# Layer-1 gathers moved into the drain and the stream's last step, and a wait for landing behind every fourth gather

## The reference

```python
def layer0(h, input, adj, weight):              # M = N = 6144, D = 128
    scores = where(adj > 0, einsum('md,de,ne->mn', h, weight, input), NEG_PAD)
    return softmax(scores / 0.07, axis=1) @ input

def layer1(h, W, a, adj):
    h = h @ W
    e = leaky_relu((h @ a[:128])[:, None] + (h @ a[128:])[None, :], 0.2)
    valid = (adj > 0) & (h.sum(axis=1) != 0)[None, :]
    att = where(valid, softmax(where(valid, e, -1e9), axis=1), 0)
    # entries under THR dropped, scaled by the number of valid neighbours
    return elu(h + attention @ h)

h = relu(layernorm(x)); x = x + layer0(h, ...)
h = relu(layernorm(x)); x = x + layer1(h, ...)
```

## Time and profile before

| | |
|---|---|
| median of 3 runs | 885.34 us (879.32 to 888.77) |
| the profiled execution's own time | 888.49 us |
| its span, first to last instruction | 886.7 us |
| mean granted TensorE clock | 0.717 of full speed |
| busy: PE, DVE, ACT, POOL | 420.1, 538.7, 389.0, 327.0 us |
| DMA packets' share of 16 engines, hardware and software queue | 49.6%, 10.7% |

### The profile page before, as it was taken

One profiled execution on the slowest core, in us unless ns is written; L12 is line 12 of the kernel. 1 busy time (PEld: TensorE's weight loads), 2 busy tenths in 40 slices (PEclk: granted clock), 3 DMA queues, 4 the chain that ended last, 5 costly groups with the idle time before them and its releaser, 6 DMA issues. The chain is left out here.

```text
span 886.7 us, 9190 instructions
## 1 busy us (share of the span) xinstructions
PE 420.1 (47%) x2773; PEld 274.2 (31%) x2806; DVE 538.7 (61%) x2015; ACT 389.0 (44%) x395; POOL 327.0 (37%) x358
## 2 busy tenths in 40 slices
PE   2356465757575656666646464632024010006564
PEld 0013223433333243434333243432023000006564
DVE  0087767767777778786859577885125020018995
ACT  4487766666575667665656624420001000001222
POOL 4003242423333232417172725556721777720000
PEclk9568786887887878696888877856555555556867
DMA  9999978878787788888979872311211222211222
GB/s 337 423 420 399 360 282 315 294 282 301 281 339 277 303 275 330 282 325 243 349 249 334 285 265 77 91 31 39 54 23 55 52 55 55 54 22 37 73 73 86
DMA packets 38037, 186.75 MB, mean 211 GB/s; under 512 B 7904, under 2 KB 9184, under 8 KB 19424
## 3 DMA queue, kind: packets, MB, share of 16 engines
q1 hardware_dynamic: 28768, 167.02, 49.6%
q0 software_dynamic: 9216, 19.11, 10.7%
HBM read 179.73 MB, written 6.37 MB: 210 GB/s over the span
## 5 line engine op out<-in xcount | busy, mean ns | idle before, releaser
L853 ACT ACTIVATE arena<-arena,half_c 128x2048 bf16<-128x2048 int32 x144 | 282.8, 1996 | 51.3 <-DMA arena<-in_adj 50.4
L788 POOL DMA_INDIRECT X<-in_L_gnn_input,idx_all x138 | 142.3, 1031 | 363.4 <-DVE idx_near L1094 325.0
L1430 PE MATMUL K<-arena,bits 128*128 128x512 bf16 x546 | 189.1, 478 | 143.6 <-ACT arena L853 130.5
L1430 PEld LDWEIGHTS K<-arena,bits 128*128 128x128 bf16 x576 | 60.6, 115 | 230.9 <-ACT arena L853 149.8
L809 POOL DMA_INDIRECT arena<-table,idx_near x96 | 91.0, 948 | 62.2 <-DMA table<-hs 33.3
L1019 DVE MAX8 keys<-K 128x8 int32<-128x128 f32 x192 | 42.5, 284 | 79.0 <-PE K L1430 70.7
L809 POOL DMA_INDIRECT E<-table,idx_near x48 | 48.8, 1016 | 14.5 <-issue 13.4
L881 ACT CAST R_all<-G 128x512 fp8e4<-128x512 f32 (+1 forms) x37 | 19.9, 575 | 69.1 <-PE G L1463 69.1
L988 ACT ACTIVATE above<-above,zero_c 128x24 f32<-128x24 f32 x6 | 1.9, 314 | 100.5 <-DVE above L1360 100.5
L1441 PE MATMUL G<-g,R_all 128*128 128x128 bf16 x333 | 32.7, 273 | 20.4 <-issue 16.0
L874 ACT CAST g<-W 128x512 bf16<-128x512 f32 (+1 forms) x13 | 7.2, 550 | 76.2 <-remote 73.9
(11 more groups left out here) (235 smaller groups left out, 995.9 us busy)
## 6 DMA issues: line engine op xcount, KB each, us to landing
arena<-in_adj SPq DMA_DIRECT2D x144, 1024.0 KB
E<-in_L_gnn_input SPq DMA_DIRECT2D x1, 3072.0 KB, 23.4
table<-hs SPq DMA_DIRECT2D x11, 262.0 KB
hs<-table SPq DMA_DIRECT2D x11, 262.0 KB, 2.8
x_all<-in_x SPq DMA_DIRECT2D x1, 2816.0 KB, 17.6
out_x<-x_all SPq DMA_DIRECT2D x11, 256.0 KB, 2.0
X<-in_L_gnn_input,idx_all POOLq DMA_INDIRECT x138
arena<-table,idx_near POOLq DMA_INDIRECT x96
```

The source lines that it names most:

```text
L788: pool.indirect_dma_start(out=x_of(b)[:, e, :], out_offset=None, in_=inp, in_offset=bass.IndirectOffsetOnAxis(ap=idx_all[:, at:at + 1], ax ...
L853: nc.scalar.activation(sign[:, load % RING, :], ring[:, load % RING, :], ACT.Sign, bias=half_c[:], scale=1.0).then_inc(signed, 1)
L1430: last = mm(bank_[:], bits[:, third * TB + j, :], sign[:, load % RING, j * FOLD:(j + 1) * FOLD], start=False, stop=(third == G - 1 and j = ...
```

## The change

Behind every fourth gather Pool waits until that gather, and those before it on its semaphore, have landed. This holds in `neighbours` and in `records`. The order of `records` changes: `records(0, 4)` goes into step 12, `records(1, 0)` and `records(1, 1)` go ahead of the last two `mean` and the last `neighbours`, the rest of third 1 and `records(0, 5)` go ahead of the wait for the whole of table 2, and only the six of third 2 stand behind it.

```diff
+    FEW = 4
...
                         ).then_inc(X_r[b], 16)
+                        if e % FEW == FEW - 1:
+                            pool.wait_ge(X_r[b], 16 * (e + 1))
...
                         ).then_inc(E_r[g][i], 16)
+                        if t % FEW == FEW - 1:
+                            pool.wait_ge(E_r[g][i], 16 * (t - i * Q + 1))
...
                         pool.wait_ge(inp_summed, 1)
                         third_stored(0)
-                    if EARLY <= n < EARLY + 4:
+                    if n >= EARLY:
                         records(0, n - EARLY)
                 pool.wait_ge(folded, T * G)
+                third_stored(1)
+                records(1, 0)
+                records(1, 1)
                 mean(NB - 2)
                 mean(NB - 1)
                 neighbours(NB - 1)
-                third_stored(1)
-                for i in range(4):
+                for i in range(2, NQ):
                     records(1, i)
+                for i in range(NB - EARLY, NQ):
+                    records(0, i)
                 third_stored(2)
-                for i in range(4):
+                for i in range(NQ):
                     records(2, i)
-                for i in range(4, NQ):
-                    for g in range(G):
-                        records(g, i)
```

## The result

The changed kernel takes **912.77 us** (median of 4 runs, 910.42 to 915.53), the kernel before 886.57 (4 runs, 879.32 to 888.77) beside it: ratio 1.031, with a 95% interval of 1.024 to 1.038. It is slower; I had forecast 849. The profiled execution took 915.53, its span 913.8.

What follows compares the result with a forecast made beforehand. It took the last gather, the rest of the freeze and 90.7 us of later computing as the bound. Third 2 at 727.7 and layer 2 from 741.0 gave 849.9, forecast 849; most of the mass between 808 and 889.

Steps and rivals of the forecast that it cites:

- The freeze and its cure: Drain and layer 2: TensorE's results get stuck while Pool issues gathers; waits behind every fourth gather cure it, margin thin.
- Rival 3: Layer 2: the freeze stays despite the waits, so computing still follows Pool's last gather; slower, 901 us; chance 0.12.
- The queue that takes 1.40 us per gather: Estimate of the freeze: Pool brings a gather each 1.25 us; runs of 80 and 38 worked off at 795.9 and 656.3.
- the price of the waits in the stream: `neighbours` in the stream: 5.3 us for each of the first two waits, 2 for the third; stream costs 23 us.
- the 12.6 of the sum: Three waits of one `neighbours` burst in the stream, added to 15.5 us of gathers and 0.3, making 28.4.
- the span of 850: Whole kernel: span from 886.7 to 850 us; execution 852, forecast 849 on the scale of the runs.
- these seven steps: Stream steps before `neighbours(7)`: each 2.5 us longer, +17.5 in all, so it starts at 412.0 instead of 394.5.
- Steps 8 to 10: Stream: Pool needs 50.2 us per step against 46 before and becomes the bound; `neighbours(10)` at 562.6 instead of 539.5.
- From `neighbours(10)` to third 2: Pool's 96 gathers 120.0 us, 23 waits 34.5, four `mean` 7.6, about 3 more: sum 165, third 2 at 727.7.
- Layer 2, from there: Step 0 taken 13.3 us behind 727.7, at 741.0; 48 gathers, 13.0 us per step of 8; end at 849.9.
- The cover of the table and of `neighbours(12)`: Drain: `neighbours(12)` lands at about 664, table ready at 694, 33 us before Pool asks for it.
- Rival 2: Stream: every wait costs 5.3 us, a step is 5.8 longer, `neighbours(10)` at 601; 888 us, no change; chance 0.14.

Runs made afterwards that it cites:

- set 1: Runs on one chip, kernel before 879.19 us: changed kernel without waits in `neighbours` 823.41, new order alone 870.82, waits alone 919.69, waits in the drain only 826.3.
- set 3: Kernels rerun on another chip, kernel before 766.58 us: changed kernel 912.76, without waits in `neighbours` 799.85, pause of some 0.3 us behind every gather instead of waits 812.51.
- set 4: Kernel before 767.69 us; changed kernel with two loads in flight 896.24, also without waits in `neighbours` 801.87; new order alone 761.2, pause behind every gather 813.56.
- sets 2 to 4: Three sets of follow-up runs, each on one chip, varying waits, pauses and loads in flight; kernel before took 763.99, 766.58 and 767.69 us.

## Why the prediction was wrong

**The freeze and its cure: right, on that kind of chip.** In set 1 the waits in `records` with the new order give 879.19 to 823.41, 6.4%, while the order alone gives 1.2% and leaves a hole of 36.3 us. `take` of steps 3 to 5 come 15.6 and 15.5 apart (14.6 forecast), and no wait over 5 us in layer 2 lacks a record. Rival 3 is out. What I did not see is that the freeze goes with the chip, or with something else that differs between the sets: the trace of one execution could not say so, and nothing here says what it is. The queue that takes 1.40 us per gather is better founded than two ends: it gave the end of the freeze in the order-alone kernel ahead of its run, to within a tenth of a us. It describes the slower kind of chip only; in set 3 a run of 118 gathers leaves nothing behind at all. What the queue is, and whether a slower rate without a wait would do as well, is not shown.

**The step that failed is the price of the waits in the stream**: "I take 5.3 for the first two waits, since the loads run then, and 2 for the third: TensorE can fold no further than the fourth load of a step before `score`, so the loads dry up". Measured 4.9, 8.1 and 7.4 in the step shown, and 5.8, 7.8 and 6.8 on average over six bursts. That is 7.8 us more than the 12.6 of the sum for each burst, 4.8 of them in the third wait and 2.5 in the second. The loads do not stop with the folds: four buffers of signs and four of rows stand behind these, and the DMA share is 1.00 until 380 us, a moment before the third group has landed. I had read the wait of TensorE and taken it for the state of the queue. That the waits in `neighbours` are the loss is shown by taking them out (set 1 and set 3); that the third is its dearest error is read from the trace, and no kernel without the third wait alone was run.

The sum, term by term, against the span of 850 that I had worked out (913.8 measured, 63.9 more):
- `score` at 36.3 behind `idx_near` instead of 29.9, a step in the stream 53.3 instead of 48.4. The first gather of `neighbours(7)` is at 454.80 instead of 412.0: **+42.8**. I had 17.5 for these seven steps; they cost 60.3 (454.80 - 394.48).
- Steps 8 to 10: 154.5 for three, where I had 150.6: **+3.9**. Each batch's waits are dearer there too (5.7, 5.9 and 5.9 in the second of them, where I had 5.3, 5.3 and 2). That Pool becomes the bound there was right.
- From `neighbours(10)` to third 2: 786.48 - 609.30 = 177.2 instead of 165.1: **+12.1**. A group of four takes 6.7 and not 6.5 us (677.67 to 684.39), 5 us on 23 waits; the rest is in the last bursts, two of whose gaps are 4.2 and 3.0.
- Layer 2, from there: 799.79 for step 0 is 13.3 behind, as forecast. To the end 114.0 instead of 108.9: **+5.1**, of which 3.2 in the first two steps, which go at Pool's pace.

The cover of the table and of `neighbours(12)` held: Pool never stopped for a table, and VectorE waits 50.6 us for third 2, as the plan had it.

**The rivals.** Rival 2 had the mechanism (dear at every wait) with 5.3 us for each, and gave 888. The runs say 6.1 on average, and 7.8 in the middle of a burst. It had only 0.14, since I took 5.3 as the upper end: it was the one landing in the earlier trace rows, the fourth of a burst with an empty queue ahead. A single row from the mildest place was used as the bound of all. The range ended at 889 for the same reason.

**The new order** brings 1.2% with the freeze (set 1) and 0.8% without (set 4). The 32 gathers that it takes from behind the table of third 2 are the likely reason; that part was not run by itself.

## What to carry to other kernels

A wait for a small transfer costs what the transfer takes while the big ones run: price it with the DMA share of exactly that stretch, and ask of every ring between load and use (here four and four buffers) how long the loads go on after the consumer has stopped. Where a wait is meant to keep something else free, put it where the path is not: here waits in `records`, with the new order, were worth 6.4% where the freeze was, and the same wait in `neighbours` cost 11% (912.8 in the result against 823.4 in set 1; 14% in set 3, 912.8 against 799.9). And before a cure is built for a stall that no record explains, run the kernel before on another chip.

## What the runs showed of the hardware that I had not expected

- **One program, two times.** The kernel before took 887 and 879 us (medians, in the result's runs and in set 1) and 764 to 768 in the other three sets. In the slower ones, VectorE gets TensorE's results up to 60 us late while Pool issues gathers without a pause. In set 3's profile the same gathers leave no such wait. A kernel that has the waits in the stream takes 912.77 and 912.76 on either kind.
- **A beat of 1.40 us.** On the slower kind the freeze ends 1.40 us per gather behind the start of a run, in three runs of two kernels (38, 80 and 48 gathers: 656.3, 795.8 and 777.8 by this rate, 654.5, 796.0 and 777.8 in the traces), and TensorE's lone matmuls start 2.80 us apart.
- **Semaphore updates are missing there.** A gather's landing raises its semaphore 16 times. The trace of the kernel before in set 3 holds 2123 updates from DMAs in its run of 118 gathers (16 for each are 1888; stores add some). The trace from the slower kind holds 291 in its run of 80 (1280 for the gathers alone), and 3802 instead of 7631 in the whole execution. Of the changed kernel's two traces, equal in time, the result's holds 6153 and set 3's 7642. This fits results that are there and are not seen; whether updates are merged on the way or only missing from the trace, the traces do not say.
- **Landing.** A gather of 128 rows lands 5.0 to 6.9 us behind its issue beside 1 MB loads (the medians of 300 to 400 us in the kernels of sets 2 to 4). In the drain a wait for it stops Pool for 2.0.
- **Depth of the loads.** Two or up to four loads of 1 MB in flight give the stream the same speed (801.87 and 799.85), with landings of 6.0 and 9.4 us for a load.
